# Two relational graph layers: per-relation sums of gathered node rows in place of a gathered table by relation

## What is computed

```python
def _rgcn_layer(x, W, self_w, b, src, dst, edge_type, num_nodes):
    xW = jnp.einsum('ni,rio->rno', x, W)
    msg = xW[edge_type, src]
    agg = jax.ops.segment_sum(msg, dst, num_segments=num_nodes)
    return agg + x @ self_w + b

h = _rgcn_layer(_layernorm(x), W1, self_w1, b1, src, dst, edge_type, 2500)
h = jax.nn.relu(h)
x = x + _rgcn_layer(h, W2, self_w2, b2, src, dst, edge_type, 2500)
```

## Time and profile before

| | us |
|---|---|
| median of 3 runs | 2281.48 (2280.98 to 2284.77) |
| profiled execution: its span | 2274.5 |
| layout of edges, statistics of x | 0 to 44 |
| table of the first layer | 44 to 187 |
| first gather stage | 187 to 626 |
| second gather stage, with counts | 626 to 1088 |
| routing | 1088 to 1134 |
| experts(0), graph layers, experts(1) | 1134 to 2275 |

### The profile page before, as it was taken

How to read it: one execution, slowest core, us unless ns; L and a number is a source line. 1 busy time by engine, 2 the same in 40 slices (tenths; PEclk the granted TensorE clock), 3 DMA queues, 4 the chain that set the end, 5 groups by cost and what they waited for, 6 DMA issues and landing times. The chain is left out here.

```text
span 2274.5 us, 37277 instructions
## 1 busy us (share of the span) xinstructions
PE 1886.6 (83%) x10428; PEld 1566.7 (69%) x10428; DVE 1208.4 (53%) x2759; ACT 1002.9 (44%) x2229; POOL 943.2 (41%) x877
## 2 busy tenths in 40 slices
PE   5996687788768878886499999579899864999997
PEld 3884476677645555554389999568688854899996
DVE  6331122122178879873555555465554565666664
ACT  1556465466365656653033333245444420233332
POOL 0115777777377777776033433220000000334332
PEclk9997899899989999998599999889999965999998
DMA  4895566665468656564535342347664556424262
GB/s 151 346 371 207 175 228 223 222 233 196 145 231 313 212 194 200 191 197 145 215 117 179 72 128 38 76 137 244 238 220 163 175 221 246 122 40 125 42 192 41
DMA packets 127195, 410.00 MB, mean 180 GB/s; under 512 B 21012, under 2 KB 60928, under 8 KB 108544
## 3 DMA queue, kind: packets, MB, share of 16 engines
q1 hardware_dynamic: 56848, 185.62, 22.2%
q0 software_dynamic: 48096, 106.74, 18.3%
q10 hardware_dynamic: 22032, 114.96, 13.4%
HBM read 256.77 MB, written 150.47 MB: 179 GB/s over the span
## 5 line engine op out<-in xcount | busy, mean ns | idle before, releaser
L2236 PE MATMUL ps<-ring,halves 128*128 x3384 | 578.8, 326 | 11.5 <-DVE halves L2303 4.0
L2236 PEld LDWEIGHTS ps<-ring,halves 128*128 128x128 f32 x3384 | 486.2, 192 | 53.8 <-issue 13.3
L1434 POOL DMA_INDIRECT ring<-tab_rel_next,gidx_relation x313 | 350.9, 1121 | 127.6 <-issue 93.9
L1126 POOL DMA_INDIRECT relation_rest<-tab_rel,gidx_relation x313 | 313.6, 1002 | 105.5 <-issue 94.5
L2345 ACT ACTIVATE x_all<-ps 128x512 f32<-128x512 f32 x188 | 113.0, 601 | 452.6 <-PE ps L2255 452.6
L1196 PE MATMUL ps<-relation_rest,slots 128*128 x784 | 214.9, 424 | 96.6 <-SPq L1041 96.2
L1526 PE MATMUL ps<-ring,slots 128*128 x784 | 202.8, 404 | 86.1 <-SPq L1311 59.5
L1893 PE MATMUL ps<-node_rows,blocks 128*128 128x512 f32 (+1 forms) x1200 | 258.5, 366 | 0.1
L1196 PEld LDWEIGHTS ps<-relation_rest,slots 128*128 128x128 f32 x784 | 161.8, 212 | 136.7 <-issue 110.0
L1526 PEld LDWEIGHTS ps<-ring,slots 128*128 128x128 f32 x784 | 147.7, 198 | 129.4 <-issue 111.0
L1893 PEld LDWEIGHTS ps<-node_rows,blocks 128*128 128x128 f32 x1200 | 203.2, 194 | 30.9 <-ACT blocks L1775 0.6
(11 more groups left out here) (281 smaller groups left out, 2770.5 us busy)
## 6 DMA issues: line engine op xcount, KB each, us to landing
ring<-split_weights SPq DMA_DIRECT2D x12, 4096.0 KB, 14.5
split_weights<-relation_rest ACTq DMA_DIRECT2D x32, 1024.0 KB, 7.1
slots<-tab_counts SPq DMA_DIRECT2D x40, 640.0 KB, 4.0
tab_rel<-relation_rest SPq DMA_DIRECT2D x20, 1024.0 KB, 5.3
tab_rel_next<-relation_rest ACTq DMA_DIRECT2D x20, 1024.0 KB, 4.7
relation_rest<-in_ffn_units ACTq DMA_DIRECT2D x16, 1024.0 KB, 5.7
split_weights<-ring ACTq DMA_DIRECT2D x16, 1024.0 KB
ring<-split_weights SPq DMA_DIRECT2D x8, 2048.0 KB, 22.8
```

The lines of the kernel that those rows point to most:

```text
L1126: nc.gpsimd.indirect_dma_start(rows[:, s * wide:s * wide + D], None, table, bass.IndirectOffsetOnAxis(ap=gidx[:, t:t + 1], axis=0)).then_i ...
L1434: nc.gpsimd.indirect_dma_start(rows[:, s * D:(s + 1) * D], None, table, bass.IndirectOffsetOnAxis(ap=gidx[:, t:t + 1], axis=0)).then_inc(g ...
L2236: ins = nc.tensor.matmul(to, lhs[left], weights(slot, right, at, n), start=first and (left, right) == (0, 0), stop=last and left == 1)
```

## The change

`run` becomes `constants`, `edge_layout`, `relational_layer(0)`, `relational_layer(1)`, `relational_again` (two blocks of fallback branches that are not taken), `route(0)`. The stage that made `tab_rel` is gone. `edge_layout` also normalises x and stores it as `tab_x` (2.6 MB). Both layers run the same code:

- POOL gathers source rows from `tab_x`, in the second layer from `tab_h`, 313 times.
- PE multiplies each edge tile by itself (`aggregate(t)`, two fp32 matmuls, gathered rows stationary, 128 columns of a one-hot of relation*16 + local destination). DVE adds each edge tile's 128 x 256 result into the sums by relation at a place that it reads into a register (`add(t)`): 313 adds a layer where there were 98.
- The sums of a node tile (18 x 144 columns less the self part: 2304 columns) live in one of three buffers. When a tile is closed (every 16 steps) PE applies the 8 relation matrices and the self matrix in 18 fp32 matmuls of 256 columns, spread over 16 steps (`products_at`). A DMA then writes zeros over the buffer (`clear`, 1.18 MB), which must land before the buffer's next tile is opened.
- Counting is spread over both layers: 44 buckets in the first, 36 in the second, one bucket in 7 steps (`SPACING`), its six pair one-hots in steps 0, 2 and 4, each with a `value_load`.
- Expert weights are split in pieces of 512 columns, 48 a layer, one every 6 steps, loaded and stored by SP. `first_lows` is gone: `route(0)` loads both halves, 16 MB.

```diff
-            self.transform(self.prep_norm, self.relation_groups(), self.tab_rel, halves=True, split=0, ...)
-            self.aggregate_and_transform()
-            self.transform_again()
...
-                self.aggregate_and_gate()
-                self.gate_again()
+            for layer in range(2):
+                self.relational_layer(layer)
+            self.relational_again()
...
+def closed(b):
+    return min(ETILES - 1, ((b + 1) * P + DRIFT - 1) // STEP)
+def opened(b):
+    return max(0, -(-(b * P - DRIFT) // STEP))
+def left_at(b):
+    return closed(b + 1) + 2 if b + 1 < TILES else closed(b) + 6
...
+                def clear(b):
+                    sp.wait_ge(out_full, b + 1)
+                    to = self.sums[:, b % SUMS * SUMW:(b % SUMS + 1) * SUMW].rearrange("p (a c) -> p a c", c=ZEROS)
+                    of = self.zero.rearrange("p (a c) -> p a c", a=1).broadcast_to([P, SUMW // ZEROS, ZEROS])
+                    sp.dma_start(to, of).then_inc(cleared[b % SUMS], 16)
...
+                def add(t):
+                    at = dve.value_load(self.at[0:1, t:t + 1], min_val=0, max_val=(SUMS - 1) * SUMW + P - 1)
+                    to = self.sums[:, bass.ds(at, SUMW)].rearrange("p (s w) -> p s w", w=KEYROW)[:, :, 0:WIN]
+                    dve.wait_ge(summed, t + 1)
+                    if t:
+                        dve.wait_ge(added, t)
...
+                    b = tile_at(opened, t)
+                    if b is not None and b >= SUMS:
+                        dve.wait_ge(cleared[b % SUMS], 16 * (b // SUMS))
+                    v.tensor_tensor(to, to, psS[t % len(psS)][:, 0:KD * P].rearrange(...), ALU.add).then_inc(added, 1)
...
+                    for j in range(0, WINDOW, 2):
+                        i = counted_at(t, j)
+                        if i is not None:
+                            at = dve.value_load(self.window[0:1, buckets[i]:buckets[i] + 1], ...)
+                            count_hots_from(i, at, j)
...
+                def aggregate(t):
+                    s, h = t % RINGROWS, t % (HOTROWS * GROUP)
+                    pe.wait_ge(hot_ready, t // GROUP + 1)
+                    if t >= len(psS):
+                        pe.wait_ge(added, t - len(psS) + 1)
+                    pe.wait_ge(gathered[s], before[s] + 16 * (t // RINGROWS + 1))
+                    for k in range(KD):
+                        last = t_.matmul(psS[t % len(psS)][:, k * P:(k + 1) * P], rows[:, s * D + k * P:s * D + (k + 1) * P],
+                                         self.onehots[:, h * P:(h + 1) * P], start=True, stop=True)
+                    last.then_inc(summed, 1)
...
+                    b, which = products_at(t)
+                    if b is not None:
+                        multiply(b, which)
+                    for j in range(0, WINDOW, 2):
+                        i = counted_at(t, j + 1)
+                        if i is not None:
+                            count_products(i, j)
```

More of the change, by code:

```diff
@@ L358, in store_x, with edge_layout @@
         return store
-    def both(self, *fetches):
-        return lambda sp, loaded: sum(f(sp, loaded) for f in fetches)
-    def edge_layout(self, fetch):
+    def edge_layout(self):
         nc, a = self.nc, self.a
@@ L383, in edge_layout @@
[L383 to L388, removed]
+            col = lambda k, n=W: self.rows[:, k:k + n]
@@ new lines, in edge_layout @@
+            raw = [col(k * W).bitcast(I32) for k in range(3)]
+            part, whole = col(3 * W).bitcast(I32), col(4 * W).bitcast(I32)
+            dstf, srcf, relf, narrowf, low, key, local, place, real = (col((5 + k) * W) for k in range(9))
+            narrows = [col(14 * W + k * NARROWS, NARROWS) for k in range(2 * ECH)]
+            sc = self.scratch
+            nmin, nmax, number, begin, near, tile, third, offset, ahead, behind, span = (sc[:, k * ECH:(k + 1) * ECH] for k in range(11))
@@ new lines, in _ @@
+                dve.wait_ge(src_ready, 1)
+                step(v.scalar_tensor_tensor(out=low, in0=low, scalar=-float(P), in1=srcf, op0=ALU.mult, op1=ALU.add))
+                v.scalar_tensor_tensor(out=key, in0=narrowf, scalar=float(KEYSTEP - NARROW), in1=key, op0=ALU.mult, op1=ALU.add).then_inc(keys_ready, 1)
+                for k in range(LOADS):
+                    dve.wait_ge(x_in[k], 16 * (1 + (k == LOADS - 1)))
+                    for i in range(k * part_tiles, (k + 1) * part_tiles):
+                        last = self.row_statistics(i)
@@ new lines, in _ @@
+                dve.wait_ge(turned, 1)
+                v.tensor_copy(self.gidx[1][:, :], ps[6][:, 0:ETILES])
+                for c in range(ECH):
+                    last = v.tensor_scalar(local[:, c * P:(c + 1) * P], dstf[:, c * P:(c + 1) * P], dstf[:, c * P:c * P + 1], None, ALU.subtract)
+                v.tensor_single_scalar(real, relf, float(REL), ALU.is_lt)
+                step(v.tensor_copy(single(begin), heads(dstf)))
+                v.scalar_tensor_tensor(out=place, in0=relf, scalar=float(WIN), in1=local, op0=ALU.mult, op1=ALU.add).then_inc(place_ready, 1)
@@ new lines, in _ @@
+                step(v.tensor_reduce(span, by_tile(local), AX.X, ALU.max))
+                v.tensor_copy(tile, whole_tile)
+                step(v.tensor_single_scalar(behind, ahead, -1.0, ALU.mult))
+                step(v.tensor_single_scalar(whole_third, tile, 43.0, ALU.mult))
+                step(v.tensor_single_scalar(whole_third, whole_third, 7, ALU.arith_shift_right))
+                v.tensor_copy(third, whole_third)
+                step(v.scalar_tensor_tensor(out=offset, in0=tile, scalar=float(SUMW - P), in1=near, op0=ALU.mult, op1=ALU.add))
@@ L435, in _ @@
+                step(v.scalar_tensor_tensor(out=offset, in0=third, scalar=-float(SUMS * SUMW), in1=offset, op0=ALU.mult, op1=ALU.add))
+                step(v.tensor_single_scalar(span, span, float(DRIFT - WIN + 1), ALU.add))
+                step(v.tensor_tensor(ahead, ahead, behind, ALU.max))
+                step(v.tensor_tensor(span, span, ahead, ALU.max))
+                v.tensor_single_scalar(span, span, -float(DRIFT), ALU.add).then_inc(bounds_ready, 1)
                 v.tensor_reduce(nmin, by_tile(narrowf), AX.X, ALU.min)
@@ L529, in over_tiles, with turn @@
                     return last
-                pe.wait_ge(compared, 1)
-                for k in range(2):
-                    last = over_tiles(ps[k][0:TILES, 0:1], lambda c: (lows[k * ECH + c][0:rows[c], :], self.ones[0:rows[c], 0:1]))
-                last.then_inc(bounded, 1)
-                pe.wait_ge(counted, 1)
-                t.matmul(ps[2][0:TILES, 0:1], from_here, groups, start=True, stop=True).then_inc(based, 1)
-                pe.wait_ge(keys_ready, 1)
-                for bank, lhs in ((5, g0), (6, srcf), (7, key), (0, low)):
+                def turn(bank, of):
@@ L1585, in _ @@
+            @block.gpsimd
+            def _(pool):
+                with self.when(pool, False):
+                    layout.gpsimd(pool)
+                    pool.wait_ge(table_ready, 1)
+                    gather.gpsimd(pool)
             @block.scalar
```

1374 lines of the change are left out of this document (635 added, 739 removed).

## The result

The change makes the kernel slower: 2358.59 us in the median (2355.85 to 2363.23) against 2281.23 (2277.6 to 2284.77), four executions each; the ratio is 1.0347, 95% interval 1.0331 to 1.0362. The prediction leaned to slower (chance 0.55; 2302, range 2228 to 2350), but with a cost of 20 us where 77 were measured; the result lies outside its range.

The account below looks back on a forecast made before the run. Both gather stages went at POOL's pace plus disturbances; now PE and DVE's mutual waits would set it. 44 + 515 + 542.5 + 6 = 1107.5 us before routing, +16, routing +4: 2294.5, plus 7.0 gives 2301.5; range 2228 to 2350.

Parts of the forecast that it names:

- the chain: Counted steps: PE and DVE wait for each other twice in two steps; 10.67 us for 7 steps, 0.85 above POOL.
- V: From the start of one DVE instruction to the next behind a register read; taken as 0.88 us.
- The clears: Zeroing a finished tile's sums by DMA: must land within 10.7 us, expected in 7.2 to 8.2; nothing booked.
- 469.5 + 15: First layer: 44 buckets at 10.67 us, plus 15 us for pieces, merges, bias adds and turns not hidden by waits.
- 4.5: Start of a layer's gathers at the meeting of the engines: 4.5 us taken, range 3 to 10.
- 384 + 42 + 15: Second layer: 36 buckets at 10.67 us, 42 us of row statistics in counted steps, and another 15 us.
- 77 + 20 + 6: Second layer's 61 steps without count, 77 us; end of the layer, 20; meetings at two skipped blocks, 6.
- Row work: Second layer's row statistics and norm: 3.0 us a tile, 14 tiles in counted steps, 42 us (20 to 60).
- From span to median: Whole kernel: the median of runs lies 7.0 us above the profiled span, so 2294.5 becomes 2301.5.
- Rival 1: Both layers: POOL keeps the pace, 7 steps cost 9.82 us, 68 us less, 2233; chance 0.37.
- Rival 2: Clears land late, so DVE's add at a newly opened buffer waits: 2346 or 2410 us; chance 0.09.
- Rival 3: DVE's one-hots and pieces lock POOL out, lengthening gathers: some 46 us more, 2348; chance 0.04.

Follow-up runs that it names:

- The first three runs: On the changed kernel: PE's count products one step later, 2316.4 us; DVE's register reads a step ahead, 2295.11 us; the two together, 2233.63 us.
- the kernel with both edits: Changed kernel with PE's count products one step later and DVE's register reads a step ahead: 2233.63 us.
- the edited kernel: Changed kernel with count products later, register reads ahead, row work spread over eight steps and clears by ScalarE: 2151.69 us.

## Why the prediction was off

- **The mechanism was right.** PE and DVE wait for each other twice in two steps and the chain, not POOL, sets the counted steps. The first three runs show it: 42, 63 and 125 us for the one link, the other and both. Where a node tile's closing and its clear are not near, the trace has the chain itself: without the six steps of each tile from its closing to the fourth after the clear, the three pairs of steps and the seventh step take 3.80, 2.97, 2.86 and 0.95 us in the first layer, 10.58 in sum; 3.80, 2.91, 2.91 and 1.05 were forecast, 10.67. V was right in the mean: from an add to the pair one-hots behind a read 0.84 us (135 cases), to the source one-hot 0.93 (63); taken was 0.88. A slip in the chain is small: two count matmuls were taken as 0.27, where its own row (12 in 1.79) gives 0.30.
- **The step that failed is "The clears": "I book nothing".** It asked only whether a clear lands in time. It does. But its transfer stretches the reads of DVE from 0.31 to about 1 us for three microseconds, in a bunch. The runs put 37 of the 57 us by which the forecast was short on it (gone with ScalarE's clears, back with zeros to DRAM). V at its mean holds such reads too, but over the chain's four reads alone; in a bunch DVE's ten reads a bucket stand in line and DVE is later than the chain (this is argued from the waits). Rows 7 showed a maximum of 1424 ns, and whose such reads were should have been asked: the trace of the kernel before already had 17 of 17 reads beside its 1 MB stores at 0.88 us or more.
- **The sum, term by term,** on the profiled executions. First bucket at 52.3 us, 48.5 predicted: +4. 44 buckets 512 against 469.5 + 15: +28. End of the first layer 23 against 26: -3. Start of the second 10.5 against 4.5: +6. 36 buckets 458 against 384 + 42 + 15 = 441: +17. From there to the start of routing 111 against 77 + 20 + 6 = 103: +8. Routing, to the first expert's matmuls, is 4 longer, as booked; the stages behind it, whose code is nearly the same, +7. Without the clears' transfers the buckets would be 44 x 11.10 = 488 and 36 x 12.27 = 442, close to the predicted 484.5 and 441. That is in part luck: in that run V is 0.83 in the mean and not 0.88, some 16 us over 80 buckets that other work has filled. Starts, ends and the stages behind make up the rest. The first gather starts at 42.9 us (46 forecast), but the first bucket only 9.4 later, and in the second layer 10.5 behind the meeting: 4.5 was taken for a start, in a range of 3 to 10.
- **Row work** was booked at 42 us. A bucket of the second layer is 1.07 us longer than one of the first, 39 us for 36; the forecast was of the right size. Spreading the work gave 24 us back in the kernel with both edits.
- **From span to median.** 7.0 us were added as before; here the median lies 2.9 below the profiled span (2361.5). That execution's own time is 2363.23, 1.7 above its span, so most of the 7.0 was scatter between executions. The second mixture's matmuls, whose code is the same, last 336 us in it against 329. So the median missed by 57 us and the span by 67.
- **Rival 1** (POOL keeps the pace) is what the edited kernel does, at 1.33 us a gather: the redesign pays once the round trip is cut. **Rival 2** looked at the clears but for the wrong effect. **Rival 3** (POOL locked out) did not come: the gather's mean in the first layer is 995 ns, below the 1121 of the earlier trace rows. The page's rule (the Trainium skill, SBUF — State Buffer, Who interferes with whom) would have the gathers longer by every one-hot's 0.44 us, if the one-hots run in the two-port mode, which no run here shows. In the trace 120 gathers overlap pair one-hots by 0.69 us in the mean and last 0.97 us, and 280 that meet none 0.95; the measurement decides.
- **The page on DMA** (the Trainium skill, DMA: Bandwidth & Descriptors, Latency and other measured facts) gives about 600 ns as a register load's floor. Here 297 ns is the least, and 0.98 us the mean beside a clear: the floor is lower and the danger is the transfer.

## What to carry to other kernels

When a loop is cut into smaller steps, count how many times two engines wait for each other in a step and what stands behind each wait; an engine whose busy share has room is still late if it is asked twice a step. Issue work that needs an answer a step after the question, and read registers ahead of the wait, not behind it. Ask of a background transfer not only whether it lands in time, but what small accesses on the critical path run while it is in flight.

## What the runs showed of the hardware

A register read of DVE lasts 0.31 us in the median. Reads that begin 1.5 to 4.5 us after the issue of a 1.18 MB transfer out of SBUF in 1 KB pieces last 0.98 us in the mean when it goes to SBUF and 0.95 when it goes to DRAM. Beside 1 MB stores of the kernel before they last 1.06, beside its 1 MB loads into SBUF 0.31. Other instructions of DVE kept their length: the 313 adds of the first layer last 405 to 426 ns, beside clears and away from them. A ScalarE activation that clears 2304 columns takes 2.11 us; with it in the clear's place 35 reads stay over 0.8 us where there were 104, with the other stores still running. Why a transfer slows the read stays open.
